# Four layers of modulated convolution and FFN on one core: the low parts of the FFN's weights all go to VectorE, and the bias sum, the wait for G's banks and layer 2's first pair are put in another order

## What is computed

```
x = x + L0_ffn(L0_cond(x, cond))   # FFN 0: fp8-rounded product + bias
x = x + L1_ffn(L1_cond(x, cond))   # FFN 1: base product + 2 of 16 experts of rank 64
x = x + L2_ffn(L2_cond(x, cond))   # FFN 2: base product + sparsemax over 8 experts of rank 16
x = x + L3_ffn(L3_cond(x, cond))   # FFN 3: rank-256 gated FFN (SiLU)

# cond: for 'same', 'upsample', 'same', 'downsample':
s = style @ mw.T + mb
weight = SCALE * w * s[:, None, :, None]
weight = weight * rsqrt(sum(weight * weight, axis=(2, 3)) + EPS)[:, :, None, None]
# then the convolution (3 taps), with a blur in the two resampling layers, + b
```

## Time and profile before

| what | value |
|---|---|
| time, median of 3 runs | 2088.21 us (2084.89 to 2093.34) |
| the profiled execution's own time | 2086.61 us |
| its span on the core | 2084.2 us |
| mean granted TensorE clock | 0.983 of full |
| TensorE busy | 1959.1 us, 94% of the span |
| VectorE busy | 1295.7 us, 62% |
| ScalarE busy | 960.2 us, 46% |
| GpSimd busy | 380.2 us, 18% |

### The profile page before, as it was taken

One profiled execution on the slowest core, in us unless ns is written; L12 is line 12 of the kernel. 1 busy time (PEld: TensorE's weight loads), 2 busy tenths in 40 slices (PEclk: granted clock), 3 DMA queues, 4 the chain that ended last, 5 costly groups with the idle time before them and its releaser, 6 DMA issues. The chain is left out here.

```text
span 2084.2 us, 32136 instructions
## 1 busy us (share of the span) xinstructions
PE 1959.1 (94%) x10201; PEld 1663.0 (80%) x10209; DVE 1295.7 (62%) x2328; ACT 960.2 (46%) x1547; POOL 380.2 (18%) x457
## 2 busy tenths in 40 slices
PE   4799978799999989998899999988999999999999
PEld 4688834799999878886788888877888878878886
DVE  6888799777767764337667667666555444444443
ACT  4488755455555431114344444434666544433442
POOL 4122212211111100002111111112121223322331
PEclk9899999999999999999999999999999999999999
DMA  7566656311122165434221221123333211142114
GB/s 192 168 191 200 178 198 227 101 60 60 60 83 68 51 192 157 141 121 161 64 69 54 69 68 59 56 81 107 101 101 102 90 46 46 52 146 85 48 45 165
DMA packets 118609, 222.30 MB, mean 107 GB/s; under 512 B 18337, under 2 KB 65185, under 8 KB 117793
## 3 DMA queue, kind: packets, MB, share of 16 engines
q1 hardware_dynamic: 102048, 212.36, 32.5%
q10 hardware_dynamic: 16512, 9.31, 1.7%
HBM read 159.04 MB, written 62.59 MB: 106 GB/s over the span
## 5 line engine op out<-in xcount | busy, mean ns | idle before, releaser
L2701 DVE SCALAR_TENSOR_TENSOR f_prod<-ps,b,f_gate 128x512 f32<-128x512 f32 (+1 forms) x88 | 66.0, 750 | 160.3 <-ACT f_gate L2641 160.3
L125 POOL TENSOR_TENSOR rows<-l_EY,ones 128x4 f32<-128x4 f32 x128 | 32.2, 252 | 730.4 <-ACT rows L1360 365.4
L2742 POOL TENSOR_TENSOR x_lo<-f_prod,x_hi 128x512 fp32r<-128x512 f32 (+1 forms) x88 | 113.7, 1292 | 277.9 <-ACT x_hi L2648 277.9
L2571 PE MATMUL ps<-pt_hi,v_hi 128*128 128x512 f32 (+1 forms) x352 | 137.5, 391 | 1.7 <-PEq L644 1.7
L2571 PE MATMUL ps<-pt_lo,v_hi 128*128 128x512 f32 (+1 forms) x352 | 137.3, 390 | 0.0
L2571 PE MATMUL ps<-pt_hi,v_lo 128*128 128x512 f32 (+1 forms) x352 | 137.2, 390 | 0.0
L2641 ACT ACTIVATE f_gate<-ps,b 128x512 f32<-128x512 f32 (+1 forms) x88 | 60.5, 687 | 155.8 <-PE ps L2571 155.8
L1583 DVE SCALAR_TENSOR_TENSOR rows<-ps,dem3e,l_middle 128x512 f32<-128x512 f32 x60 | 45.1, 751 | 120.5 <-ACT l_middle L1329 97.7
L1097 PE MATMUL ps<-l_u_hi,l_g_hi 128*128 128x512 f32 x272 | 111.7, 411 | 5.9 <-DVE l_g_lo L1617 5.7
L125 POOL TENSOR_TENSOR XE<-rows,ones 128x8 f32 (+1 forms) x96 | 21.9, 250 | 511.4 <-DVE rows L1793 254.3
L1097 PE MATMUL ps<-l_u_lo,l_g_hi 128*128 128x512 f32 x272 | 108.7, 400 | 0.0
(11 more groups left out here) (408 smaller groups left out, 5800.1 us busy)
## 6 DMA issues: line engine op xcount, KB each, us to landing
x<-rows SPq DMA_DIRECT2D x64, 512.0 KB, 2.9
xin<-x SPq DMA_DIRECT2D x96, 256.0 KB, 4.0
rows<-x SPq DMA_DIRECT2D x48, 512.0 KB, 4.1
out<-rows SPq DMA_DIRECT2D x32, 512.0 KB, 2.6
v<-in_ffn_v SPq DMA_DIRECT2D x84, 128.0 KB, 2.6
xin<-in_x SPq DMA_DIRECT2D x16, 512.0 KB, 5.9
xb<-in_x SPq DMA_DIRECT2D x16, 512.0 KB, 3.3
x<-xb SPq DMA_DIRECT2D x16, 512.0 KB, 2.6
```

The costliest lines, as they stand in the source:

```text
L2571: mm = nc.tensor.matmul(ps[0:m, 2 * g + gu, :], v1sp[ws][:, s, r, gu, 0:m], pt[ms][:, r, cols], start=(k == 0), stop=(k == 5))
L2701: v.scalar_tensor_tensor(prod[0:m, g, :], ps[0:m, 2 * g + 1, :], b1[0:m, 1, bass.ds(2 * i + g, 1)], gate[0:m, g, :], ALU.add, ALU.mult).th ...
L2742: nc.gpsimd.tensor_tensor(asp[1][0:m, g, :], prod[0:m, g, :], asp[0][0:m, g, :].bitcast(F32), ALU.subtract).then_inc(al_ready, 1)
```

## The change

- `POOL_CHUNKS` is 0: VectorE makes the low parts of chunks 0 to 2 too. It still takes one chunk, two chunks and the rest at the same three places, so that these are now chunk 0, chunks 1 and 2, and chunks 3 and up. GpSimd makes none.
- The bias sum of pair p, where a pair follows, also waits for `sum_c(p+1)`: it can run only between the sums and the split of the next pair's G.
- Layer 1: `weights_g` waits for `x_part` (banks 5 and 6 read) and no longer for `xo_ready` (bank 7 read as well), and `tail` on VectorE reads banks 5 and 6 first, and `small` from bank 7 behind them.
- First pair of layers 1 and 2 on VectorE: behind `split_c(1)` come `differ_u(1)`, `read_u_fast(1)`, `read_a(2)`, `split_z(3)`, `split_x(2)`. In layer 2, `sum_c(1)` is ahead of `gates(0)`, and the split of the gated vector (`split_gt(0)`) is drawn ahead on both engines: behind `differ_u(1)` on VectorE, behind `read_u_fast(1)` on ScalarE.

```diff
-POOL_CHUNKS = 3
+POOL_CHUNKS = 0
...
                 if with_ffn and not (isinstance(p, int) and p < 2):
-                    pe.wait_ge(xo_ready, r0 + p - 1)
+                    pe.wait_ge(x_part if layer == 1 else xo_ready, r0 + p - 1)
...
                 if fast:
                     split_gc(1)
-                    lead(1, 3)
+                    read_u_fast(1)
+                    if layer == 2:
+                        split_gt(0)
+                    read_a(2)
+                    split_z(3)
+                    split_gaps(1)
+                    split_x(2)
                 if layer > 0:
                     tail(0)
...
+            def split_gt(p):
+                dve.wait_ge(side[2], side0[2] + p + 1)
+                v.tensor_tensor(gsp[1][:, :], ps[:, 7, 3 * P:4 * P], gsp[0][:, :].bitcast(F32),
+                                ALU.subtract).then_inc(side[3], 1)
+                dve.wait_ge(side[3], side0[3] + p + 1)
+                v.tensor_copy(tau[:, 0:1], tau[:, 0:1]).then_inc(small_read, 1)
...
                     dve.wait_ge(ffn_done, r0 + p + 1)
-                    v.tensor_copy(kept["small"][:, :], ps[:, 7, REST:THIRD]).then_inc(small_read, 1)
                     dve.wait_ge(xr_biased, r0 + p + 1)
...
                     v.tensor_tensor(x2, ps[:, 5:7, 0:THIRD].rearrange("p c (m s) -> p s c m", s=2), x2,
                                     ALU.add).then_inc(x_part, 1)
+                    v.tensor_copy(kept["small"][:, :], ps[:, 7, REST:THIRD]).then_inc(small_read, 1)
...
                     if fast:
                         some_chunks(len(chunks))
-                        if layer == 2:
-                            gates(0)
                         if layer > 1:
                             wait_lo(dve, len(chunks) - 1)
                         sum_c(1)
+                        if layer == 2:
+                            gates(0)
                     split_g(1)
                     if fast:
                         split_c(1)
                     some_chunks(len(chunks))
                     if fast:
-                        lead(1, 3)
+                        differ_u(1)
+                        if layer == 2:
+                            split_gt(0)
+                        read_u_fast(1)
+                        read_a(2)
+                        split_z(3)
+                        split_x(2)
                     tail(0)
...
                 if with_ffn:
+                    if ahead:
+                        pool.wait_ge(sums_ready, 2 * (f0 + p) + 3)
                     pool.wait_ge(xr_loaded, 16 * (r0 + p + 1))
                     g.tensor_tensor(xr[:, :], xr[:, :], bias[:, :], ALU.add).then_inc(xr_biased, 1)
```

More of the change, by code:

```diff
@@ L1380, in tail @@
                     route_exp(nc, act, kept, p - 1, sem)
-                if layer == 2:
-                    act.wait_ge(side[1], side0[1] + p + 1)
-                    nc.scalar.activation(gsp[0][:, :], ps[:, 7, 3 * P:4 * P], ACT.Copy).then_inc(side[2], 1)
+                if layer == 2 and not (isinstance(p, int) and p == 0):
+                    split_gt(p)
                 if layer == 3:
@@ L1386, in tail @@
                     nc.scalar.activation(pr[:, :], ps[:, 7, 0:RANK], ACT.Copy).then_inc(side[0], 1)
+            def split_gt(p):
+                act.wait_ge(side[1], side0[1] + p + 1)
+                nc.scalar.activation(gsp[0][:, :], ps[:, 7, 3 * P:4 * P], ACT.Copy).then_inc(side[2], 1)
             def tail_p(p):
```

## The result

The changed kernel takes 2073.34 us, the median of ten runs from 2070.82 up; the kernel before, ten runs interleaved with them, 2083.66 (2072.65 to 2093.34). The ratio is 0.9949, 95% interval 0.9924 to 0.9974: faster by 10.3 us. One run of the changed kernel (3866.11 us) and one of the kernel before in the last set of experiments (2748.08 us) were disturbed; the ratios leave them out, the medians given do not, and without them those medians are 2072.67 and 2085.01 us. The forecast was 2070.5, range 2061 to 2081. The runs before lie within 21 us, those after within 5; that difference of spread turned out to be the key.

The account below looks back on a forecast made before the run. TensorE, busy 94% of the span, was taken as the bound, so edits pay only where it stands still or runs at its lower clock. -17.3 - 2.4 + 3.8 + 3.5 - 3.7 = -16.1 from 2086.6: 2070.5 us, range 2061 to 2081.

Parts of the forecast that it names:

- Part 1: Later pairs: bias sum behind `sum_c` ends six long `sum_c`, saving TensorE waits of 10.9 us and 6.4 of clock: -17.3 us.
- rival 3: The load of x decides the bias sum's start; only half the collisions typically occur: sum -7.4, 2079 us; chance 0.05.
- The clock term: Matmuls at TensorE's lower clock behind a standstill: 1.6 us in four of the six long-`sum_c` pairs, 6.4 us.
- The bias sum beside what follows: Later pairs: in its new place the bias sum delays nothing TensorE waits for, covered by ScalarE's activations before `split_g`; cost nothing.
- rival 4: The bias sum holds `split_g(p+1)` in every pair, up to 2.4 us each: slower, 2098 us; chance 0.04.
- Part 2: Layer 1: `weights_g` no longer waits for bank 7's last read or the small copy; eight waits go: -2.4 us.
- Part 3, layers 1 and 2: First pairs: VectorE makes GpSimd's low parts, edges' gain eaten, later chunks late: +3.8 us in layer 1, +3.5 in layer 2.
- The chain through chunk 5: First pairs, layers 1 and 2: chunk 5's load, waiting for slot 1, holds `read_h(0, 0)`, eating the edges' gain: +0.2 us.
- The smaller wait forecast at L1205: Layer 2's first pair: TensorE waits at L1205, reached at 1008.5 us for 1006.8, smaller than its wait at L1191.
- Layer 3, -3.7: First pair: edges 3.5 us earlier, chunk 0 costs 0.6, about 0.8 back from conv0 at full clock: -3.7 us.
- Rival 1: First pairs' late chunks cost more, +6.5 and +6 us, and the bias sum's gain is -12.5: 2081 us; chance 0.17.
- Rival 2: First pairs come out better, loads at the lower bounds: -26 us, 2061 us; chance 0.16.

Follow-up runs that it names:

- e2: The changed kernel without the bias sum's new wait for `sum_c`: 2079.79 us, ratio 0.9997 to the kernel before.
- e1: The kernel before with the bias sum's new wait for `sum_c` alone: 2067.47 us, ratio 0.993.
- e10: The changed kernel with an extra GpSimd multiplication of the bias by one, begun when `sum_g` is done, beside `sum_c` in each pair: 2114.70 us, ratio 1.0137.
- e6: The changed kernel with one more low part on VectorE ahead of the last edges in the first pairs: 2062.26 us, ratio 0.9889.
- e8: The changed kernel with three low parts of each layer on GpSimd again: 2065.99 us, ratio 0.9924.
- e4: The kernel before with only layer 1's G behind two banks and VectorE's new tail: 2079.58 us, ratio 0.9991.
- e5: The kernel before with the bias sum held until `sum_g` is done, meant to force collisions with `sum_c`: 2082.89 us, ratio 1.001.
- e3: The kernel before with no low part on GpSimd, alone: 2087.08 us, ratio 1.0025.
- e7: The changed kernel with layer 1's G behind all three banks and the old tail: 2073.89 us, ratio 0.997.
- e12: e9 without layer 1's G behind two banks and the new tail: 2060.44 us, ratio 0.9885.
- e9: The changed kernel with three low parts on GpSimd in layers 1 and 2 and none in layer 3: 2059.28 us, ratio 0.9894.
- e11: The changed kernel with two low parts on GpSimd in layers 1 and 2 and none in layer 3: 2059.06 us, ratio 0.9875.

## Why the prediction was right, and where it was not

The time fell inside the range and 2.8 us from the number, faster as forecast. Its mechanisms were mostly right; one step failed and one was mis-sized. The gain was overstated by 5.8 us (16.1 for 10.3), and the execution that the sum was made against, 2086.6, lay 2.9 above the median of the ten runs, which took half of that back.

**Part 1, -17.3.** The mechanism is shown, by taking the wait away (e2), by adding it alone (e1) and by forcing a collision in nearly every pair (e10). The prediction misread one thing: the bias sum did not always start "just before" `sum_c`; in three of the six pairs it started 0.21 to 0.24 us behind. In the profiled executions it is worth what I summed: layer 2's rest falls by 11.6 us with four long sums gone, layer 1's by 6.2 with two (e1). Over the five versions without the wait, layer 2's rest lies 33.4 us in all above the 379.33 of e1, for twelve long sums, 2.8 each. The size failed for the median. The step was in rival 3: "the three times before lie within 0.4%, so the count hardly varies." The five profiles without the wait have 6, 4, 4, 3 and 2 long sums, and the median gain of the wait is 13.5 us (e1), of which 2.0 are layer 1's first pair, not the 17.8 of the two rests in one profile. I worked from one execution with many collisions. An estimate from 2.8 us each and those 2.0: the 29 times of before in e1's set, 2073.5 to 2088.5, lie above e1's 2067.5 by one to seven of them. That no collision is left fits the narrow spread, but is not all of it: e6 and e8 have none in their profiles and spread over 8.5 and 6.5 us. The sum was right for the one execution that it was made on.

The clock term (1.6 us in four of the six) was worked out from one period. Six holds of 2.2 us in layer 2's later pairs, in four traces, stand apart and have the next period in full. In three the period is 27.3 us for 25.1, as much longer as the hold, and the granted clock over it is 1.00 (before at 1276 us, e4 at 1268, e5 at 1066). In the other three it is 28.6, and the granted clock reads 0.94 (before at 1018 and 1097, e3 at 1027). So the term is real, 1.3 us, and comes with half of these holds. In e10 it does not come: the period is 1.66 us longer for a hold of 1.70, with a granted clock of 1.00 in 1100 to 1340 us. What decides stays open.

**The bias sum beside what follows** was costed at nothing in the later pairs. In layer 2 that holds: it starts 0.94 us behind `sum_c` in nearly all pairs and ends within 0.15 us of `split_g`'s start, which takes its 1.41. In layer 1 it does not quite. Here are `split_g` and the tail in one pair after, and the same pair before:

```profile
557.77 0.76 DVE L1603 TENSOR_TENSOR b_raw<-l_g_f 128x256 f32<-128x256 f32 x2
561.00 2.22 DVE L1621 SCALAR_TENSOR_TENSOR l_g_lo<-l_g_f,s_u,l_g_hi 128x512 fp32r<-128x512 f32 x2 [1.00 <-ACT l_pairs_hi L1353]
...
573.80 0.92 DVE L1789 TENSOR_TENSOR rows<-ps,rows 128x736 f32<-128x736 f32 x1
```
```profile
556.64 0.76 DVE L1594 TENSOR_TENSOR b_raw<-l_g_f 128x256 f32<-128x256 f32 x2
559.87 1.42 DVE L1612 SCALAR_TENSOR_TENSOR l_g_lo<-l_g_f,s_u,l_g_hi 128x512 fp32r<-128x512 f32 x2 [1.00 <-ACT l_pairs_hi L1353]
...
572.04 0.91 DVE L1774 TENSOR_TENSOR rows<-ps,rows 128x736 f32<-128x736 f32 x1
572.99 0.46 DVE L1778 TENSOR_TENSOR rows<-ps,rows 128x288 f32<-128x288 f32 x1
```

`split_g` takes 0.80 us more. That is the mechanism of rival 4, at 0.8 us of its 2.4, and in layer 1 alone.

**Part 2, -2.4: the step that failed.** "The eight waits were at most 0.4 us, and those two reads take longer than that." I took a wait for the length of the reads that it skips and did not ask what VectorE does with the time. Counted from `sum_c`, G was released before by the last read, at 573.45 - 556.64 = 16.8 us; after, by the first sum, at 574.72 - 557.77 = 16.95. The copy and the last read came out of the chain, and a longer `split_g` went in. In this pair VectorE reaches its tail behind its own other work, not behind a wait for TensorE's `ffn`, so the tail comes as late as VectorE does, and so does G. The three comparisons (e4 against before, e7 against the changed kernel, e12 against e9) all show no difference. Nor do the stretches: of the versions with the wait, the rest of layer 1 takes 353.0 us on average in the five with the new tail (after, e6, e8, e9, e11) and 352.9 in the three without (e1, e7, e12). The new tail itself makes x come late. e4 adds nothing else, and in most of layer 1's pairs its bias sum starts 1.6 to 1.8 us behind `sum_c`, for 0.6 to 1.6 before; e7 takes it away, and there it is mostly 0.9 to 1.4, for 1.3 to 2.5 after. The longer `split_g` goes with it: 1.9 us or more in most of layer 1's pairs of the versions that have the new tail (after, e2, e4, e6, e8, e9, e11), mostly under 1.8 in e1, e7 and e12. What it costs lies under a microsecond and stays open.

**Part 3, layers 1 and 2.** +4.66 and +3.25 for +3.8 and +3.5. The chain through chunk 5 came as worked out: forecast of `read_h` about 33 us into the layer, measured 33.0, with a DMA as the releaser. e6 confirms it as the main cause: with that load released sooner, the time drops. Behind `split_h` the last low part ended 9.4 us later for 8.4. In layer 2 the order of events was mostly as forecast: the wait at L1191 and the bias sum on `split_g` (3.53 us). The smaller wait forecast at L1205 is not there; 1.8 us stand at L1116 instead:

```profile
1001.51 2.42 POOL L2025 TENSOR_TENSOR rows<-rows,l_bias 128x1024 f32<-128x1024 f32 x1 [19.98 <-DMA rows<-x]
```
```profile
997.96 0.29 DVE L1747 COPY l_small<-ps 128x136 f32<-128x136 f32 x1
...
1001.61 3.53 DVE L1621 SCALAR_TENSOR_TENSOR l_g_lo<-l_g_f,s_u,l_g_hi 128x512 fp32r<-128x512 f32 x2
```

But the sums hid two larger terms of opposite sign. The versions make a square of low parts (on GpSimd or not) by order (old or new). Layer 1, free of the bias sum's hold: 51.64 and 58.61 in the old order (e1, e3), 51.95 and 58.34 in the new. Layer 2: 62.31 and 69.55, 58.33 and 65.69. So the late low parts cost 6.4 to 7.0 us in layer 1 and 7.3 in layer 2; the new order is worth nothing in layer 1 (forecast +0.5) and -3.9 in layer 2. In layer 2 the late parts look like a threshold and not a price per sum: with two of the three on GpSimd (e11), or with none and one made earlier (e6), it takes 58.9 us, near e8's 58.3; in layer 1 e6 keeps 1.8 us of the price. In layer 1, 2.0 of the price was masked: the hold on the old low parts (5.71 for 3.49) went away at the same time, and I booked it inside this part.

**Layer 3, -3.7.** 36.4 to 37.9 us in the eight versions of the table without low parts on GpSimd there (mean 37.3), 39.9 to 41.4 in the five with (mean 40.3): -2.9, inside its bounds. The medians of e8 and e9 differ by 6.7, more than this.

**Behind layer 3's first pair** I had nothing, and the profile after has +3.7 us. No line of the change is there. All versions fall at 642.3 to 643.4 or 644.5 to 646.1, with the same work. In e8 against e9 the difference arises in two places, 1.4 us near 1650 and 1.6 near 2040, where the granted clocks differ (windows; columns: length, busy time of each engine, clock, DMA share, GB/s), e8 and then e9:

```profile
2020.00:2040.00 20.00, 19.29 (x75) 13.44 (x74) 7.10 (x7) 6.30 (x9) 3.89 (x4) 0.91 0.12 47
```
```profile
2020.00:2040.00 20.00, 19.29 (x83) 14.25 (x82) 7.96 (x8) 4.68 (x6) 2.56 (x2) 1.00 0.13 53
```

The granted clock sorts all thirteen versions of the table. In the windows 1635:1675 and 2025:2055 it reads 0.96 and 0.94 in after, e1, e6, e8 and e11 (645.3 to 646.1 us), 0.96 in the first alone in e4 (643.4), 0.94 in the second alone in e5 (644.5), and 0.99 or 1.00 in the others (642.3 to 642.9). So the +3.7 us of the profile after go with two short stretches at the lower clock. Why an execution has them is not settled, nor whether the kernels have them equally often; this may be the rest of e9's 6.7 us.

**Rivals.** Rival 1 (late chunks dearer) came near the price and was wrong about the total, since the new order paid for half of it in layer 2 and the bias sum's hold went away in layer 1. Rival 2 did not come. Rival 3 gave the right reason for the lower gain, at 0.05, and its own sentence against it was the error. Rival 4 was there in layer 1 at 0.8 us in `split_g`, and cannot be seen in the layer's length.

The best that was timed is e9 or e11, 2059 us: the wait, layer 2's new order, and low parts off GpSimd in layer 3 only. Moving one sum forward (e6) makes the full change nearly as fast, 2062. A version with e9's settings and that sum forward was not tried.

## What to carry to other kernels

A hold between two engines whose onset hangs on a DMA's landing by tenths of a microsecond does not cost a fixed time but a number of hits that differs from run to run; look at the spread of the times before you multiply one profile's count, and price the cure against the median. Ask what a wait's end is released by after the edit, not how long the instructions are that it no longer covers: if the releasing engine gets there as late as before, the wait stays. Where work is moved from one engine to another in a first pair, follow the buffer slots: one sum moved forward into idle time was worth 11 us in two layers, 7 of them because a load hung on it. And sum the parts of a change apart, since a loss of 14 us (the late low parts) under larger gains can look like one good number.

## What the runs showed of the hardware

GpSimd's multiplication with a broadcast column, 2.13 us, holds a VectorE sum of two SBUF operands as the bias sum of 2.42 us does: 0.76 becomes 2.46 in 28 of 28 pairs. The Trainium skill (SBUF — State Buffer, Who interferes with whom) says of the pair of SBUF ports that GpSimd and VectorE share that the one that issues first keeps it for its whole instruction. The trace agrees for e10, where GpSimd's row starts 0.05 us behind the first of the two VectorE sums and ahead of the second, and VectorE's rows end 0.28 us behind GpSimd's end at 1070.36. A sum with one operand in PSUM was not held: in the profile after, `split_h` at 1222.74 us takes 1.22 us beside a bias sum that has run since 1222.65 and runs to 1225.08, as it does alone.

How fine the onset is: in the profile before, `sum_c` is long in the six later pairs in which the bias sum starts between 0.83 us ahead of it and 0.24 behind, and short in all in which it starts 0.39 us behind or later. It goes the other way too: where the bias sum starts 0.39 us behind, at 1126.22 us, `sum_c` takes its 0.76, and the bias sum takes 2.66 us for 2.42.
